# Top-two expert selection in a two-layer Mamba and mixture-of-experts kernel: row maxima and comparisons over all tiles of a front in place of MAX8 and FIND_INDEX8 per tile

## The reference

```
scores = softmax(xt @ gate_w.T)            # 8 per token
topk_w, topk_i = jax.lax.top_k(scores, 2)
comb = zeros((T, 8)).at[arange(T)[:, None], topk_i].add(topk_w)
y = sum over e of comb[:, e:e+1] * swiglu(xt, w1[e], w2[e], w3[e])
```

## Time and profile before

| | |
|---|---|
| median of 3 runs | 1181.41 us (1178.0 to 1184.15) |
| profiled execution | 1182.9 us |
| its span, first to last instruction | 1181.1 us |
| busy: DVE | 960.9 us (81%), 1811 instructions |
| busy: PE | 916.1 us (78%) |
| busy: ACT, POOL | 608.5 us (52%), 592.5 us (50%) |
| mean granted TensorE clock | 0.870 |

### The profile page before, as it was taken

The page is one execution under the profiler, slowest core; times in us unless marked ns, Lnnn a source line. Parts: engine busy times, 40 slices in busy tenths (PEclk is TensorE's granted clock), DMA queues, the critical chain, the costliest instruction groups (busy, mean ns, idle before and its releaser), DMA issues.

```text
span 1181.1 us, 16955 instructions
## 1 busy us (share of the span) xinstructions
PE 916.1 (78%) x4540; PEld 650.3 (55%) x4540; DVE 960.9 (81%) x1811; ACT 608.5 (52%) x1593; POOL 592.5 (50%) x415
## 2 busy tenths in 40 slices
PE   3475687967767778868888888888768888898588
PEld 1343475645645655656656565656546565566455
DVE  3797889899889897987999978998479877876463
ACT  2444545654545555545575556654455455555133
POOL 1348226657427544781358543765848365226300
PEclk9576889988888998998999899998887889889677
DMA  9944335456344534563536534566454464445000
GB/s 280 294 119 127 87 89 123 118 126 186 86 100 120 125 90 114 150 183 91 114 99 151 132 93 117 133 189 147 114 124 93 103 169 114 104 91 146 21 24 13
DMA packets 168650, 144.71 MB, mean 123 GB/s; under 512 B 15680, under 2 KB 135536, under 8 KB 168560
## 3 DMA queue, kind: packets, MB, share of 16 engines
q10 hardware_dynamic: 39776, 67.47, 26.1%
q1 hardware_dynamic: 121104, 60.43, 18.0%
q0 software_dynamic: 7680, 15.74, 4.2%
HBM read 106.88 MB, written 36.70 MB: 122 GB/s over the span
## 4 chain that ended last, share of the span: by engine, by line
PE 35%; DVE 33%; issue 14%; ACT 9%; POOL 6%; DMA 1%; ACTq 1%; another core or an unknown queue 1%; DVEq 0%; SPq 0%; POOLq 0%
DVE pA L1352 11%; PE pM L935 6%; PE pH L845 4%; PE pM L925 4%; DVE hj L1388 4%; POOL dBx L748 3%; PE pG L897 3%; PE p L900 3%; PE pU L898 3%; DVE hj L1400 2%; ACT pA L955 2%; DVE hc L1360 2%; PE pG L900 2%; PE pH L913 2%; POOL rows_in L706 1%
## 5 line engine op out<-in xcount | busy, mean ns | idle before, releaser
L748 POOL TENSOR_TENSOR dBx<-dtx,bcb 128x1024 f32<-128x1024 f32 (+1 forms) x144 | 304.6, 2115 | 403.6 <-DVE pA L1352 387.0
L845 PE MATMUL pH<-const,hc 128*128 128x128 f32 x1024 | 160.9, 304 | 43.4 <-DVE hc L1360 38.9
L1352 DVE TENSOR_TENSOR_SCAN pA<-pA,carry,dBx 128x512 f32<-128x512 f32 (+1 forms) x160 | 162.9, 1063 | 30.9 <-ACT pA L955 24.9
L955 ACT ACTIVATE pA<-dt,am 128x512 f32<-128x512 f32 (+1 forms) x288 | 173.9, 639 | 17.6 <-DVE hc L1360 9.4
L1352 DVE TENSOR_TENSOR_SCAN pA<-pA,dBx 128x512 f32<-128x512 f32 x128 | 149.8, 1216 | 27.9 <-ACT pA L955 11.7
L925 PE MATMUL pM<-const,hj 128*128 128x128 f32 (+3 forms) x636 | 131.9, 305 | 44.3 <-ACT hT L1138 10.7
L845 PEld LDWEIGHTS pH<-const,hc 128*128 128x128 f32 x1024 | 128.1, 156 | 64.3 <-DVE hc L1360 46.1
L1360 DVE TENSOR_TENSOR hc<-pA,bcb 128x1024 f32<-128x1024 f32 (+1 forms) x144 | 159.3, 1106 | 5.0
L706 POOL DMA_INDIRECT rows_in<-xn,slots x120 | 127.8, 1065 | 30.1 <-issue 27.0
L925 PEld LDWEIGHTS pM<-const,hj 128*128 128x128 f32 (+3 forms) x636 | 74.0, 141 | 118.9 <-issue 88.7
L1135 ACT ACTIVATE yj<-pM 128x128 f32<-128x128 f32 x236 | 65.4, 277 | 140.1 <-PE pM L935 125.0
(11 more groups left out here) (201 smaller groups left out, 1533.5 us busy)
## 6 DMA issues: line engine op xcount, KB each, us to landing
bcb<-bc_rows ACTq DMA_DIRECT2D x112, 512.0 KB
rows_out<-yj SPq DMA_DIRECT2D x236, 64.0 KB
xg<-rows_in SPq DMA_DIRECT2D x176, 64.0 KB
bcb<-bc_rows ACTq DMA_DIRECT2D x32, 256.0 KB
rows_in<-gy SPq DMA_DIRECT2D x8, 512.0 KB, 8.9
mixed<-s_st SPq DMA_DIRECT2D x12, 256.0 KB
so<-rows_out SPq DMA_DIRECT2D x6, 512.0 KB
sr<-mixed SPq DMA_DIRECT2D x6, 512.0 KB
```

The source lines that it names most:

```text
L748: pool.tensor_tensor(dBx[:, N % 2, :, 0:t1 - t0], dtx[q % 2][:, :, t0:t1], row, ALU.mult).then_inc(dBx_ready, 1)
L845: last = mm(pH[:, half, c * DI + k * P:c * DI + (k + 1) * P], hc[:, N % 2, k, t * P:(t + 1) * P], ident, is_transpose=True, start=(n == 0 ...
L955: A(pA[:, k, 0:t1 - t0], dt[q % 2][:, k, t0:t1], ACT.Exp, scale=am[:, k, n:n + 1]).then_inc(decay_ready, 1)
L1352: dve.tensor_tensor_scan(pA[:, k, 0:w], pA[:, k, 0:w], dBx[:, N % 2, k, 0:w], carry[:, k, N % NS:N % NS + 1] if N in carry_after else 0.0, ...
```

## The change

The per-tile MAX8 and FIND_INDEX8 go, with their tiles `top`, `idx`, `idf`. For each of the two experts, five instructions over all tiles of the front take their place, each linked: the row maximum straight into the weights tile, comparison of `pr` with it, multiplication by the constants 8 to 1 (so that among equal ones the lowest expert counts highest), the row maximum of that, and comparison with it, which is the one-hot mask. After the first expert its probability is lowered by 2. The copy of the weights in layer 0 goes.

```
-                    for c in range(c0, c1):
-                        last = dve.max(top[:, c, :], pr[:, c, :])
-                    link(last)
-                    for c in range(c0, c1):
-                        last = dve.max_index(idx[:, c, :], top[:, c, :], pr[:, c, :])
-                    link(last)
-                    link(dve.tensor_copy(idf[:, cs], idx[:, cs, 0:TOPK]))
-                    io = iota8.rearrange("p (o e) -> p o e", o=1).broadcast_to([P, c1 - c0, NE])
+                    w = wts[l][bb][:, cs]
+                    down = from8.rearrange("p (o e) -> p o e", o=1).broadcast_to([P, c1 - c0, NE])
                     for k in range(TOPK):
-                        last = dve.tensor_tensor(oh[:, k, cs], io, idf[:, cs, k:k + 1].broadcast_to([P, c1 - c0, NE]), ALU.is_equal)
-                    link(last)
+                        link(dve.tensor_reduce(w[:, :, k], pr[:, cs], op=ALU.max, axis=AX))
+                        link(dve.tensor_tensor(hit[:, cs], pr[:, cs], w[:, :, k:k + 1].broadcast_to([P, c1 - c0, NE]), ALU.is_equal))
+                        link(dve.tensor_tensor(hit[:, cs], hit[:, cs], down, ALU.mult))
+                        link(dve.tensor_reduce(se[:, cs], hit[:, cs], op=ALU.max, axis=AX))
+                        link(dve.tensor_tensor(oh[:, k, cs], down, per_token(se[:, cs], NE), ALU.is_equal))
+                        if k == 0:
+                            link(dve.scalar_tensor_tensor(out=pr[:, cs], in0=oh[:, 0, cs], scalar=-2.0, in1=pr[:, cs], op0=ALU.mult, op1=ALU.add))
...
-                    w = wts[l][bb][:, cs]
-                    if l == 0:
-                        link(dve.tensor_copy(w, top[:, :, 0:TOPK]))
-                    else:
-                        link(dve.tensor_reduce(se[:, cs], top[:, cs, 0:TOPK], op=ALU.add, axis=AX))
+                    if l:
+                        link(dve.tensor_reduce(se[:, cs], w, op=ALU.add, axis=AX))
                         link(dve.reciprocal(se[:, cs], se[:, cs]))
-                        link(dve.tensor_tensor(w, top[:, cs, 0:TOPK], per_token(se[:, cs], TOPK), ALU.mult))
+                        link(dve.tensor_tensor(w, w, per_token(se[:, cs], TOPK), ALU.mult))
```

More of the change, by code:

```diff
@@ L367, in program @@
         ident, not_before, ones = (const[:, k * P:(k + 1) * P] for k in range(3))
-        iota8 = const[:, 3 * P:3 * P + NE]
+        from8 = const[:, 3 * P:3 * P + NE]
         steps128 = const[:, 3 * P + NE:3 * P + NE + NE * CT]
@@ L395, in program @@
         pr = sb("pr", [P, CT, NE])
-        top = sb("top", [P, CT, 8])
-        idx = sb("idx", [P, CT, 8], U32)
-        idf = sb("idf", [P, CT, 2])
+        hit = sb("hit", [P, CT, NE])
         oh = sb("oh", [P, TOPK, CT, NE])
@@ L1501 @@
     arrays["const"] = np.ascontiguousarray(np.concatenate([
-        np.eye(P), np.triu(np.ones((P, P)), 1) - 1, np.ones((P, P)), row * np.arange(NE), row * np.tile(P * np.arange(CT), NE),
+        np.eye(P), np.triu(np.ones((P, P)), 1) - 1, np.ones((P, P)), row * (NE - np.arange(NE)), row * np.tile(P * np.arange(CT), NE),
         row * np.arange(TILES),
```

## The result

| | before | changed |
|---|---|---|
| median of 20 runs each, us | 1179.17 (1165.42 to 1184.78) | 1187.91 (1184.52 to 1195.80) |
| ratio, 95% interval | 1 | 1.0095 (1.0071 to 1.0118) |
| profiled execution, its span, us | 1182.9, 1181.1 | 1184.8, 1183.0 |
| mean granted clock of the profiled execution | 0.870 | 0.872 |

The change costs 0.95%, 11.2 us of 1181.41, where 3.8 were forecast. The ratio on record is not that of the two medians: these differ by 8.7 us, 0.74%, which its interval still contains. Like all ratios here, it leaves out runs more than 1.5% above the fastest of their kernel. The median itself lies within the range of 1178 to 1190, but only because 20 runs put the kernel before at 1179.17 and not at 1181.41; the difference is what counts, and its lower bound, 0.71% or 8.4 us, is above everything that the prediction had as its own case (5.5 at most).

A forecast was written before the change was run, and what follows sets the result against it. No single engine was taken to bound the kernel: its chain was PE 35%, DVE 33%. Seven fronts on the chain (3 x 0.15, 0.33, 0.81, 1.12, 1.09) added 3.8 us to the median of 1181.41: 1185.2, range 1178 to 1190.

The forecast's parts named there:

- its own case: Whole kernel: 1185.2 us from the fronts' prices, own range 1183 to 1187.5, chance 0.50; upper bound of the sum 5.5 us.
- Where the change sits, and its price in each front: Routing blocks, on the chain in seven of ten fronts: 2.84 us wide, 2.47 with four tiles, 2.30 with two.
- the 269 kept as an upper bound: Multiplications in wide fronts: 225 ns expected, 269 ns at most, +0.13 us for a wide front.
- The cover of (0,0) and (1,1): Fronts (0,0), (1,1), (1,2): 0.8 us hidden by PE and ACT work; without that cover the sum is 4.6.
- The rule weighed: Routing blocks: advice of fewer operations, not fewer semaphores, would give about -5 us; the prediction went by the trace, +3.8.
- the rival of cheap links: New DVE instructions: linked starts as cheap as unlinked, 0.14 us apart, -4.8 us (1176.6) or -7.9 (1173.5); chance 0.04.
- the sum: Seven fronts on the chain: their added times, 0.15 to 1.12 us each, together make the kernel 3.8 us longer.
- term (1,5): Last front, two tiles: 2.30 us against 1.21, counted as 1.09 us on the chain.
- Absorbed: Delays vanish in DVE's next waits for ACT or PE: +1.9 us if half, +0.5 if nearly all; 1182, chance 0.17.
- The stall of (1,2) goes: Front (1,2): 4.7 us of unknown waits vanish with the short-instruction burst, -0.9 us in all, 1180.5; chance 0.10.
- More waits in a stalled stretch: Front (1,2): seven more linked instructions each start 0.65 us late, 4.5 us more, 8.3 in all, 1189.7; chance 0.12.
- Phase, not price, decides: Whole kernel: total moving by more than the fronts' own differences; shifts of phase between engines, to either side, had 0.07.

The follow-up runs named there:

- b4: Kernel before, with row maxima replacing the search in front (1,5) alone; ratio 1.0032 (1.0007 to 1.0058), 3.7 us.
- e3: Kernel before, with five useless linked DVE multiplications of 16 elements added in front (1,5); ratio 1.0041 (1.0006 to 1.0077), 4.8 us.
- d1: Kernel before, with row maxima in nine fronts and the search kept in (1,5); ratio 1.0040 (1.0011 to 1.0070), 4.7 us.
- b2: Changed kernel with 12 extra matmuls in two PE gaps of (1,5); ratio to the kernel before 1.0051 (1.0026 to 1.0076).
- c1: Kernel before, unchanged, run again as its own neighbour on the same chip; ratio 1.0004 (0.9978 to 1.0031).
- a2: Kernel before with the old instructions, but its tiles placed as in the changed kernel; ratio 1.0001 (0.9976 to 1.0026).
- b3: Kernel before without search and cast: MAX8 kept, probabilities compared with its two first results; ratio 0.9975 (0.9952 to 0.9997).
- a1: Changed kernel run again, against the kernel before on the same chip; ratio 1.0077 (1.0048 to 1.0106).
- d4: Kernel before with the combination parts of sequence 2 in layer 1 one step later; ratio 0.9992 (0.9966 to 1.0018).
- b1: Kernel before with 12 extra matmuls in two PE gaps of (1,5); ratio 0.9944 (0.9913 to 0.9975).
- d2: Kernel before with 12 extra matmuls in two PE gaps of (1,5), a second time, on another chip; ratio 0.9978 (0.9950 to 1.0007).

## Why the prediction was wrong

**Where the change sits, and its price in each front: right in the main.** Forecast 2.84, 2.47 and 2.30 us, measured 2.82, 2.52 and 2.28. The groups of the changed kernel (line, form, count, busy us, mean ns) have 220 and 219 ns for the row maxima, where 220 and 211 were taken, and 225 for the multiplication, so the 269 kept as an upper bound was not needed:

```profile
L1239 DVE TENSOR_TENSOR hit<-hit,const 128x64 f32<-128x64 f32 x14 | 3.1, 225 | 0.5
...
L1238 DVE TENSOR_TENSOR hit<-pr,wts 128x64 f32<-128x64 f32 x14 | 3.1, 225 | 0.5
L1237 DVE TENSOR_REDUCE wts<-pr 128x8 f32<-128x64 f32 x14 | 3.1, 220 | 0.5
L1240 DVE TENSOR_REDUCE se<-hit 128x8 f32<-128x64 f32 x14 | 3.1, 219 | 0.5
...
L1243 DVE SCALAR_TENSOR_TENSOR pr<-oh,pr 128x64 f32<-128x64 f32 x7 | 1.6, 224 | 0.2
```

The instruction count of 1695 came as forecast, and the chain through the new lines of (1,4) and (1,5); in (1,3) it came in two of three profiles. The cover of (0,0) and (1,1), counted as hidden, is gone in all three: by the prediction's own prices that is 0.5 us more, a small part of what is missing.

**The rule weighed: the row was right.** Linked starts are 0.25 to 0.26 apart in the changed kernel too. By the rule of the Trainium skill (VectorE: DVE Perf Modes, section Rules for kernel authors) fewer operations should have paid. This trace disagrees: a wide block became 2.82 us long instead of 2.51, and the rival of cheap links is out.

**The step that failed: the sum, in its term (1,5).** "On the chain: ... (1,5) 1.09" counts a microsecond on the chain as one microsecond of the kernel. The front did become 1.07 us longer, but that delay costs 3.7 us alone (b4), 4.8 with other instructions in its place (e3), together 4.1 give or take 2.4, and 4.4 to 6.5 as the whole less d1. The other nine fronts, 2.7 us by the sum and 3.5 with their cover gone, measured 4.7 (1.3 to 8.3), which doesn't contradict it. So 2.6 to 5.4 us of the 5.3 to 7.4 that the forecast lacks sit in the one term that the prediction itself had marked, in its remarks on the rivals, as the place where the chain goes on into gates and matmuls.

**Why that term is larger.** If every other duration and the order of everything stayed, making DVE 4.6 us longer in all could not make the kernel more than 4.6 us longer. The measured 9.1 to 11.2 is twice that, so something else changed. What the profiles show to differ is PE: 67 to 81 us busy for the same matmuls in the tail, and up to 8 us between executions from the gate behind (1,5) to the end. The mean clock falls in all five kernels that delay (1,5) and stays in five of the six listed that don't. That is support, but no proof. The fill neither kept the clock from falling nor brought the distance surely down; b2 is slower at a higher clock; and within one kernel a fall of 0.008 goes with 1.1 to 2.0 us and not with 6. Shown is that about 1.1 us in this place cost more than itself, 1.7 to 6.5 us. That the clock is what multiplies it is the explanation that fits most of this, but the cause stays open, and so does whether the stretches from (1,3) on add to it.

**The rivals.** *Absorbed* is out: the opposite happened. *The stall of (1,2) goes* is not what happened, but its premise is only half wrong: the stall comes and goes with the search, and wasn't seen without it. Wrong is its worth. From `pr` of (1,2) to that of (1,3) the kernel before took 105.4 us with the late starts, and 104.1 (c1) and 103.2 (a2) without: at most 2.2 us of the 4.7. *More waits in a stalled stretch* came nearest in time (1189.7), but by a mechanism that isn't there: the new linked instructions in (1,2), and those behind them that started late before, start on time, as the rows of DVE's timeline show, with no idle time in brackets:

```profile
847.02 0.23 DVE L1238 TENSOR_TENSOR hit<-pr,wts 128x64 f32<-128x64 f32 x1
...
849.34 0.23 DVE L1241 TENSOR_TENSOR oh<-const,se 128x64 f32<-128x64 f32 x1
...
850.35 0.20 DVE L1253 RECIPROCAL se<-se 128x8 f32<-128x8 f32 x1
...
850.79 0.17 DVE L1256 TENSOR_SCALAR sg<-sg 128x8 f32<-128x8 f32 x1
```

"Phase, not price, decides" was named as what would make the prediction wrong. It had a chance of 0.07 with no mechanism. What to look for was the engine that waits longest behind the edit, and how long its work takes afterwards.

## What to carry to other kernels

Don't count a delay on the chain as its own length without a look at the engine that waits for it. Here PE stood idle 6 us behind the edit and then ran at changing clock, and a microsecond cost about four; look at the granted clock of the stretch behind such a wait in several executions. A gain on the chain may be worth less than its length, as in b3. Before replacing several short unlinked instructions by fewer linked ones, count what a linked one takes from start to start (here 0.21 us at 16 elements, 0.26 at 64): even with eight tiles to share them the eleven lost 0.31 us. And take the worth of half a per cent from many runs, never from one pair of profiles.

## What the runs showed of the hardware

Eleven linked DVE instructions took 2.82 us with 64 elements in a partition and still 2.28 with 16: a quarter of the data saves a fifth of the time. An unlinked pair of the search is much cheaper: in e3 the second search of a front starts 0.13 us after the first (1100.99, then 1101.12).

TensorE's granted clock in the tail was between 0.69 (a1) and 0.84 (d1) in the 13 profiles without extra matmuls, and the tail's length between 89.2 (d4) and 103.2 us (a1). The same instructions alone spread over several us: 92.2 (a2) and 98.0 (c1), 89.6 (b1) and 97.1 (d2). Across all 20 profiles each us at half clock in the tail went with 0.34 us of length. That is a relation between single executions, and within one kernel's runs the total follows its clock much less.

Twelve extra matmuls in PE's gaps raised the mean granted clock of the kernel before on both chips (0.8870 to 0.8980, 0.8846 to 0.8915), but gave no gain in time that is clear of the spread.
